# Offset stage of a convolution with deformable sampling: regroup the offsets after all the rows, and share the row copies otherwise over three DMA queues

## The reference, cut to what matters

```
x = x + L0(_gn(x))    # two 3x3 convolutions 32 -> 16, batch norm, a 3x3 attention map with a sigmoid
x = x + L1(_gn(x))    # deformable 3x3 convolution 32 -> 32
# L1, for each pixel and each of the 9 taps k:
offs = conv3x3(x, offset_w) + offset_b          # 18 channels: y and x offset of each tap
mask = 2 * sigmoid(conv3x3(x, mod_w) + mod_b)   # 9 channels
sampled = bilinear(x, y + off_y + ky, x + off_x + kx) * mask
out = einsum('nckhw,ock->nohw', sampled, w) + bias
out = relu(batch_norm(out))                     # mean and variance over images and pixels
```

## Time and profile before

| | |
|---|---|
| median of three runs | 480.02 us |
| the profiled execution | 479.59 us |
| its span in the trace | 477.8 us |
| PE busy | 344.6 us (72%) |
| DVE busy | 332.2 us (70%) |
| ACT busy | 269.0 us (56%) |
| POOL busy | 156.3 us (33%) |
| mean granted TensorE clock | 0.859 of full speed |
| sampling loop | about 194 to 436 us |

### The profile page before, as it was taken

One profiled execution on the slowest core, in us unless ns is written; L12 is line 12 of the kernel. 1 busy time (PEld: TensorE's weight loads), 2 busy tenths in 40 slices (PEclk: granted clock), 3 DMA queues, 4 the chain that ended last, 5 costly groups with the idle time before them and its releaser, 6 DMA issues.

```text
span 477.8 us, 14528 instructions
## 1 busy us (share of the span) xinstructions
PE 344.6 (72%) x6057; PEld 217.8 (46%) x6058; DVE 332.2 (70%) x625; ACT 269.0 (56%) x508; POOL 156.3 (33%) x218
## 2 busy tenths in 40 slices
PE   0089999495251933899979999979999789992550
PEld 0022334121110311677766777757777567772450
DVE  5363348806440582599995999939999599997156
ACT  1022333113210342889886989958898689893344
POOL 8910000663440000244442444414444235445100
PEclk9988999987655565999997999979999899998565
DMA  6895100575614233210000100001000000000004
GB/s 205 176 233 138 29 1 0 149 175 140 150 38 95 71 92 80 58 43 25 25 25 2 43 25 25 25 4 41 25 20 9 24 5 3 3 3 8 12 1 176
DMA packets 18707, 28.66 MB, mean 60 GB/s; under 512 B 6998, under 2 KB 7573, under 8 KB 18629
## 3 DMA queue, kind: packets, MB, share of 16 engines
q1 hardware_dynamic: 13765, 21.02, 16.5%
q0 software_dynamic: 1632, 3.45, 3.3%
q10 hardware_dynamic: 3246, 3.27, 3.0%
HBM read 8.03 MB, written 5.83 MB: 29 GB/s over the span
## 4 chain that ended last, share of the span: by engine, by line
DVE 51%; PE 22%; SPq 11%; DMA 6%; issue 4%; ACT 2%; ACTq 2%; POOL 1%; DVEq 1%; POOLq 0%
DVE prod L1309 27%; DVE areg L1317 18%; SPq L340 5%; PE ps L582 4%; PE ps L603 4%; SPq L435 4%; PE ps L652 3%; DMA prod<-xpad 2%; PE ps L593 2%; ACTq L340 2%; PE ps L780 2%; SPq L415 2%; PE ps L715 2%; DMA x_sb<-in_x 1%; PE ps L639 1%
## 5 line engine op out<-in xcount | busy, mean ns | idle before, releaser
L559 POOL TENSOR_TENSOR prod<-prod 128x288 f32<-128x288 f32 x128 | 99.9, 801 | 195.1 <-DVE prod L1309 195.1
L1309 DVE TENSOR_TENSOR prod<-ps,hy 128x480 f32<-128x480 f32 (+1 forms) x256 | 139.3, 600 | 33.7 <-PE ps L780 33.7
L780 PE MATMUL ps<-zreg,hx 64*64 64x96 f32 x4608 | 135.9, 252 | 14.9 <-DVE prod L1309 14.9
L780 PEld LDWEIGHTS ps<-zreg,hx 64*64 64x64 f32 x4608 | 112.7, 135 | 34.0 <-DVE prod L1309 26.1
L931 ACT ACTIVATE hx<-ps 128x576 f32<-128x576 f32 x131 | 78.1, 648 | 54.0 <-PE ps L771 30.2
L937 ACT ACTIVATE hx<-hx,rbias 128x576 f32<-128x576 f32 x131 | 95.6, 795 | 0.0
L1317 DVE TENSOR_REDUCE areg<-prod 128x32 f32<-128x576 f32 x128 | 92.6, 747 | 0.9 <-POOL prod L559 0.9
L639 PE MATMUL ps<-preg,sel 26*128 26x288 bf16 x260 | 44.4, 292 | 14.4 <-DMA preg<-wreg 11.7
L1013 ACT ACTIVATE zreg<-ps 128x288 f32<-128x288 f32 x128 | 46.1, 424 | 0.0
L771 PE MATMUL ps<-wzp,sreg 128*128 128x144 bf16 x512 | 44.5, 232 | 0.0
L960 ACT ACTIVATE sreg<-ps,offbc 128x512 f32<-128x512 f32 x8 | 5.5, 687 | 63.5 <-PE ps L652 42.7
(11 more groups left out here) (177 smaller groups left out, 339.3 us busy)
## 6 DMA issues: line engine op xcount, KB each, us to landing
scratch<-zreg SPq DMA_DIRECT2D x12, 240.0 KB, 4.2
sreg<-scratch SPq DMA_DIRECT2D x12, 192.0 KB, 2.5
out<-x_sb SPq DMA_DIRECT2D x8, 256.0 KB, 2.1
areg<-xpad SPq DMA_DIRECT2D x30, 66.0 KB, 2.4
x_sb<-in_x SPq DMA_DIRECT2D x3, 512.0 KB, 4.8
sreg<-scratch SPq DMA_DIRECT2D x4, 336.0 KB, 3.3
hx<-xpad SPq DMA_DIRECT2D x18, 66.0 KB, 4.0
zreg<-xpad SPq DMA_DIRECT2D x18, 66.0 KB, 2.1
```

Of the source, the lines that this page charges most:

```text
L559: pool.tensor_tensor(slots[:, :, 0:2 * KK], slots[:, :, 0:2 * KK], slots[:, :, 4 * KK:6 * KK], ALU.add).then_inc(folded, 1)
L780: return pe.matmul(g_ps(g, h)[u * W:(u + 1) * W, k - TAPS[h][0], :, :], hx[s, (t + u) % 4, k, :], z_sb[s, y + u + k // 3:y + u + k // 3 + ...
L1309: mul = vector.tensor_tensor(pv[:, n0:n1], gv, wv[:, n0:n1], ALU.mult)
```

## The change

1. Rows are numbered n = 3·b + dy, and each queue gets a range of the 12. First convolution: SP 0 to 3, ACT 4 to 7, POOL 8 to 11 (4/4/4 where it was 6/3/3). Second: SP 0 to 4, ACT 5 and 6, POOL 7 to 11 (5/2/5 where it was 6/3/3). PE's counts follow.
2. SP issues rows of 3 ahead of store 0, rows of 5 ahead of store 1, and all rows, 6 and 7 too, ahead of the first regrouping.
3. Quarters 0 and 1 are regrouped together by 9 DMAs of twice the size, when both have been saved; so there are 27 regroup DMAs in place of 36. Store 2 comes behind them. Load 0 comes next, then regroup 2 (as DMAs 10 to 18), store 3, regroup 3, and the other loads.
4. The waits on `px_ready` are counted down by 9. DVE waits once for the last split of GpSimd (xparts_low) before the sampling loop.

```diff
+        SYNC_ROWS, ACT_ROWS, POOL_ROWS = range(0, 4), range(4, 8), range(8, 12)
+        SYNC_ROWS2, ACT_ROWS2, POOL_ROWS2 = range(0, 5), range(5, 7), range(7, 12)
+
+        def replicate(eng, c, rows, homes, done):
+
+            for n in rows:
+                b, dy = n // 3, n % 3
                 r = c * CH_ROWS + PAD_T - 1 + dy
                 eng.dma_start(homes[c][dy * C:(dy + 1) * C, b, :],
                               xpad[b * C:(b + 1) * C, r:r + CH_ROWS, :].rearrange("c r x -> c (r x)"))\
-                    .then_inc((last if b == B - 1 else ready)[c], 16)
-
-        def replicate2(eng, c, b):
+                    .then_inc(done[c], 16)
+
+        def replicate2(eng, c, rows, done=rep2_ready):
 
             eng.wait_ge(norm2, c + 1)
             if REUSES[c] is not None:
                 eng.wait_ge(cv_ready, REUSES[c] + 1)
-            replicate(eng, c, b, xrep2, rep2_ready, rep2_last)
+            replicate(eng, c, rows, xrep2, done)
...
             for c in range(NCH):
                 sync.wait_ge(norm1, (c + 1) // 2 + 1)
-                replicate(sync, c, 0)
-                replicate(sync, c, 1)
+                replicate(sync, c, SYNC_ROWS, xrep, xrep_ready)
...
-            def regroup_offsets(q):
+            def regroup_offsets(q0, q1, counted, taps=range(KK)):
+
                 n = 2 * CH_ROWS * W
-                g, at = q // 2, q % 2 * n
-
-                sync.wait_ge(px_ready, 16 * (1 + q * PX_DMAS))
-                sync.wait_ge(tp_saved, q + 1 + CREDIT)
-                for k in range(KK):
-                    sync.dma_start(px[g * NXP:(g + 1) * NXP, k, at:at + n],
-                                   tpart[k * NXP:(k + 1) * NXP, q * n:(q + 1) * n]).then_inc(px_ready, 16)
+                g, at = q0 // 2, q0 % 2 * n
+
+                sync.wait_ge(px_ready, 16 * (1 + counted))
+                sync.wait_ge(tp_saved, q1 + CREDIT)
+                for k in taps:
+                    sync.dma_start(px[g * NXP:(g + 1) * NXP, k, at:at + (q1 - q0) * n],
+                                   tpart[k * NXP:(k + 1) * NXP, q0 * n:q1 * n]).then_inc(px_ready, 16)
 
             def rows_for(*chunks):
 
                 for c in chunks:
-                    for b in range(2):
-                        replicate2(sync, c, b)
-
-            rows_for(0, 1, 2)
+                    replicate2(sync, c, SYNC_ROWS2)
+
+            rows_for(0, 1, 2, 3)
             store_parts(0)
-            rows_for(3, 4)
+            rows_for(4, 5)
             store_parts(1)
-            rows_for(5)
-            regroup_offsets(0)
-            rows_for(6)
+            rows_for(6, 7)
+            regroup_offsets(0, 2, 0)
             store_parts(2)
-            rows_for(7)
-            regroup_offsets(1)
 
             sync.wait_ge(off_ready, NCH)
             sync.wait_ge(xparts_stored, 16 * B * (NQ - 1))
             load_piece(0, 0)
+            regroup_offsets(2, 3, PX_DMAS)
             store_parts(NQ - 1)
+            regroup_offsets(3, 4, 2 * PX_DMAS)
             for q in range(1, NQ):
-                if q < 3:
-                    regroup_offsets(NQ - 3 + q)
...
             for c in range(3):
-                replicate2(pool, c, B - 1)
+                replicate2(pool, c, POOL_ROWS2, rep2_last)
             pool.wait_ge(norm2, NCH)
             split_low_rows(0)
-            replicate2(pool, 3, B - 1)
-            replicate2(pool, 4, B - 1)
+            replicate2(pool, 3, POOL_ROWS2, rep2_last)
+            replicate2(pool, 4, POOL_ROWS2, rep2_last)
             split_low_rows(1)
...
-                pe.wait_ge(rep2_ready[c], 16 * 3 * (B - 1))
-                pe.wait_ge(rep2_last[c], 16 * 3)
+                pe.wait_ge(rep2_ready[c], 16 * (len(SYNC_ROWS2) + len(ACT_ROWS2)))
+                pe.wait_ge(rep2_last[c], 16 * len(POOL_ROWS2))
...
-            pe.wait_ge(px_ready, 16 * (1 + 3 * PX_DMAS))
+            pe.wait_ge(px_ready, 16 * (1 + 2 * PX_DMAS))
             distance(0, 0, PAIR_BANKS[0])
...
             for c in range(NCH // 2):
                 act.wait_ge(norm1, (c + 1) // 2 + 1)
-                replicate(act, c, 2)
+                replicate(act, c, ACT_ROWS, xrep, xrep_ready)
             root(1)
...
                 if 3 <= c + 2 < NCH:
-                    replicate2(act, c + 2, 2)
+                    replicate2(act, c + 2, ACT_ROWS2)
                 save_conv2(c)
...
             vector.wait_ge(hy_ready, NQ * 3)
+            vector.wait_ge(xparts_low, NQ)
```

More of the change, by code:

```diff
@@ L334, in conv_deform_kernel @@
         block = ctx.enter_context(nc.Block())
-        def replicate(eng, c, b, homes=xrep, ready=xrep_ready, last=xrep_last):
-            for dy in range(3):
+        SYNC_ROWS, ACT_ROWS, POOL_ROWS = range(0, 4), range(4, 8), range(8, 12)
[3 more added lines that the diff above has]
+                b, dy = n // 3, n % 3
                 r = c * CH_ROWS + PAD_T - 1 + dy
@@ L500, in _ @@
                 pool.wait_ge(norm1, (c + 1) // 2 + 1)
-                replicate(pool, c, 3)
+                replicate(pool, c, POOL_ROWS, xrep, xrep_last)
             def split_low_rows(q):
@@ L521, in _ @@
             for c in range(3):
-                replicate2(pool, c, B - 1)
+                replicate2(pool, c, POOL_ROWS2, rep2_last)
             pool.wait_ge(norm2, NCH)
             split_low_rows(0)
-            replicate2(pool, 3, B - 1)
-            replicate2(pool, 4, B - 1)
+            replicate2(pool, 3, POOL_ROWS2, rep2_last)
+            replicate2(pool, 4, POOL_ROWS2, rep2_last)
             split_low_rows(1)
-            replicate2(pool, 5, B - 1)
-            replicate2(pool, 6, B - 1)
+            replicate2(pool, 5, POOL_ROWS2, rep2_last)
+            replicate2(pool, 6, POOL_ROWS2, rep2_last)
             split_low_rows(2)
-            replicate2(pool, 7, B - 1)
+            replicate2(pool, 7, POOL_ROWS2, rep2_last)
             split_low_rows(3)
@@ L565, in _ @@
             pool.wait_ge(reach_ready, 2)
-            pool.wait_ge(px_ready, 16 * (1 + NQ * PX_DMAS))
+            pool.wait_ge(px_ready, 16 * (1 + 3 * PX_DMAS))
             far_rows(pool, lambda b, y, n: None, far_stage)
@@ L575, in conv_chunk @@
             def conv_chunk(c, u):
-                pe.wait_ge(xrep_ready[c], 16 * 3 * (B - 1))
-                pe.wait_ge(xrep_last[c], 16 * 3)
+                pe.wait_ge(xrep_ready[c], 16 * (len(SYNC_ROWS) + len(ACT_ROWS)))
+                pe.wait_ge(xrep_last[c], 16 * len(POOL_ROWS))
                 rows = xrep[c].rearrange("p b (r x) -> p b r x", x=XC)
@@ L758, in _ @@
                         if t == CH_ROWS:
-                            pe.wait_ge(px_ready, 16 * (1 + NQ * PX_DMAS))
+                            pe.wait_ge(px_ready, 16 * (1 + 3 * PX_DMAS))
                     pe.wait_ge(dist_ready, t + 3)
@@ L914, in _ @@
                     act.wait_ge(norm1, (c + NCH // 2 + 1) // 2 + 1)
-                    replicate(act, c + NCH // 2, 2)
+                    replicate(act, c + NCH // 2, ACT_ROWS, xrep, xrep_ready)
                 save_branches(c, c % 2)
@@ L971, in _ @@
             for c in range(3):
-                replicate2(act, c, 2)
+                replicate2(act, c, ACT_ROWS2)
             act.wait_ge(late_loaded, 16 * NLATE)
```

## The result

The changed kernel takes 447.57 us (median of 4 runs, 443.76 to 448.61) where the kernel before takes 478.14 (4 runs): a ratio of 0.938, 95% interval 0.927 to 0.949. That is 30.6 us less, where 25.3 were forecast; 447.6 lies in the range, near its lower end. Medians are of all runs of a kernel, ratios only of the runs in its faster state, so a ratio is not quite the quotient of two medians.

A forecast was written before the change was run, and what follows sets the result against it. Offset stage bound by waits in SP's queue, not transfer rate; the start by needed rows coming last. 22.1 us (offset stage) plus 3.2 (first convolution) make 25.3 off 479.59: 454.3 us, range 446 to 465.

The forecast's parts named there:

- (a): Start of the offset stage: chunk 0 of the second convolution starts at 94.2 us, where it was 95.44.
- (d): Offset stage: store 1 goes at 117.4 us, and chunk 6 starts at 128.1 in place of 152.95.
- (c): Offset stage: DVE's second split ends at 117.4 us, not 120.47; chunks 3, 4, 5 start at about 107.5, 115, 121.
- The sign of being wrong: Offset stage: PE waiting over 2 us for chunk 4 or 5 would show the forecast wrong.
- (e): Chunk 6 to regrouping: 7.25 us to ready for chunk 7, then 7.0; quarter 1 saved at 142.3, not 168.0.
- (f): SP's path from quarter 1's save to the first distance: 22.5 us, first distance at 164.9 where it was 186.97.
- step (b): Chunks 0 to 2 of the offset stage: chunk 2 ends at 105.6 us, DVE's first offsets 3.1 us sooner.
- The first convolution: Start of the kernel: chunk 1 starts at 27.6 us, when `attw` is made, in place of 30.80; 3.2 us.
- rival 1: Offset stage's regrouping: large regroup DMAs cost double, 6.4 us more, total 460.7 us; chance 0.10.
- rival 2: First convolution: transfer rate alone sets chunk 1, which stays at 30.80; total 457.5 us; chance 0.15.
- rival 3: Offset stage: transfers become the bound, at 150 GB/s chunk 6 starts 9.6 us later; total 463.9 us; chance 0.10.
- Rival 4: Sampling loop: low clock adds 2 us a pair; 518 us if half the loop ran so; chance 0.03.

The follow-up runs named there:

- order_only: SP's new order and the joint regrouping, with the old 6/3/3 shares in both convolutions, against the kernel before: 456.52 us, ratio 0.963.
- store_first: The changed kernel with store 2 issued ahead of the joint regrouping: 446.0 us, ratio 0.946 to the kernel before.
- split_regroup: The changed kernel with store 2 at once on SP and the regrouping spread over POOL, SP and ScalarE: 441.64 us, ratio 0.937 to the kernel before.
- before_paced2: The kernel before with 46, 80 and 16 full-size float32 matmuls on idle operands ahead of the waits for chunks 5, 6, 7: 478.96 us, ratio 1.008.
- after_again: The changed kernel run and profiled once more, unaltered: 451.16 us, ratio 0.950 to the kernel before.
- share1_only: The kernel before with rows shared 4/4/4 in the first convolution only: 472.91 us against 478.62, ratio 0.990.
- warm_start: The changed kernel with ten 512-column matmuls on loaded data ahead of the first convolution's first chunk: 451.7 us, ratio 0.950 to the kernel before.
- split_paced: `split_regroup` plus 12 matmuls ahead of the first convolution, 14 and 30 float32 ones ahead of the second's chunks 4 and 6: 440.66 us.
- before_paced: The kernel before with 30, 52 and 10 26-row matmuls on idle operands ahead of the waits for chunks 5, 6, 7: 487.58 us, ratio 1.023.

## Why the prediction was right, and where its size was off

**The cause is right.** SP's queue held ready buffers empty behind store 1 and regroup 0. With the order alone turned round, the stage is 23.7 us shorter (`order_only`). Chunk 6 was put at 41.3 us behind the second normalization and came at 41.4 and 42.6; in the first profile steps (a) to (d) each hold within 1.1 us, in the second within 1.8. In (c) DVE's split ended 1 us late: one of its casts took 1.78 us in place of 0.80 while POOL's second split ran beside it. In (d) the five rows behind the store went 1 us sooner and made it good; this was luck, for in the second profile they did not. The sign of being wrong that came true, PE waiting over 2 us for chunk 4 (4.56 and 3.33), comes from PE's pace, as the miss in (e) does: chunk 3 took 2.78 us in these profiles and not the 4.92 of before, so PE was ready sooner, and chunk 4 started no later than forecast.

**Step (f)** is right to 0.4 us: from regrouping to first distance 22.16 us in place of 22.5, with the new wait at 3.2 as written. `store_first` shows that the wait was on the path, and `split_regroup` that SP's issuing was: spread over three queues, (f) takes 12.9 us, 9.2 less, and what is left is bound by DVE's last parts to within 0.87 us.

**Step (e) was mis-sized, the main miss of the offset stage.** It said that from the start of chunk 6 to ready for chunk 7 are 7.25 us and from there to regrouping 7.0, as the rows of before show, 14.25 together. Measured: 4.36 + 4.93 = 9.3 in the first profile, 5.9 + 4.9 = 10.8 in the second. I read 5.35 and 4.81 us off as the price of a chunk. They are the price of a chunk after PE has idled 15.30 us, and of the next one, still slow after 0.84 us more: the same has chunk 1 at 2.75. With all rows sent ahead chunk 7 follows chunk 6 after at most 0.54 us, and it takes 2.78 in every profile of the new order; its turns and the parts' turning go at that pace too; chunk 6 itself is fast or slow by how long PE has waited. I used the 2.75 in step (b) and not here. That is 3.4 to 5.0 us. `before_paced2` shows it in the old order too: with chunk 7 at 2.78 regrouping starts 4.9 us behind it and not 7.0.

**The first convolution: 3.2 us forecast, 5.1 and 5.4 measured.** The new shares acted in the direction forecast, but through another number: chunk 1 did not wait for `attw` (made at 26.9, with chunk 1 at 28.2), and chunk 0 came at 23.1 and not 22.2, so chunk 1, which now only waits for PE to finish chunk 0 at its slow pace, gained only 2.6 us. The other 2.5 came behind it, where PE, with the gap of 1.55 us gone, was at its fast pace earlier. Chunk 1, the first attention product and chunk 2 took 3.58, 1.10 and 2.78 us where they had taken 4.16, 2.02 and 3.77. The sum had carried the shift through unchanged "by PE's unbroken work".

**The total.** The profile lost 35.8 us for the 25.3 of the sum. Of the 10.5 us between, 5.0 are (e), 1.9 the first convolution, 0.2 the small misses of the other steps, and 3.4 the spread behind the first distance, which is luck. In `after_again`, 28.6 us, the last is 1.4 us the other way.

**The rivals.** Large DMAs cost no more (rival 1 out: 714 ns either way). The rate does not decide chunk 1 (rival 2 out, `share1_only`). The transfers were not the bound (rival 3 out): chunk 6 was on time. That rival was priced 1.8 us low: 72 rows of 66 KB and two stores of 0.96 MB are 6.7 MB, not 6.4. From 87 to 124 us the changed kernel moved 194 GB/s. Rival 4, the slow pace in the loop, did not come in the changed kernel's first pairs, 3.04 us each; it came in other kernels, for one pair in `before_paced2`, `store_first`, `warm_start` and `split_regroup` and for two in `split_paced`, at 1.5 to 2.2 us a pair, for which I had put 2. A shorter wait is not its condition: in `warm_start` PE waited 11.57 us ahead of the first distance, about as in the kernel before.

**Joined DMAs** were priced as part of (f) with nine issues. That they save nothing against eighteen, since quarter 0's find cover, I had not seen; it changes no term of the sum.

## What to carry to other kernels

Look in a DMA-issuing queue for ready work that stands behind a wait for something later: here two such places cost 24 us of a 480 us kernel, and they show as long PE waits for a transfer that itself took 2 us. A duration read off the trace holds only under its own circumstances: if a change removes the idle time ahead of an instruction, price it by a row of the same instruction that follows work directly. After changing the waits ahead of a stage, look at the first instructions of the next stage, where the gain may be given back.

## What the runs showed of the hardware

- PE's pace follows what it did before. In all profiles the 24 matmuls of a chunk in the second convolution took 4.48 to 5.35 us when PE had idled 2.91 us or more right ahead of them. They took 2.75 to 2.78 us in most other cases, after waits of up to 2.17 us. The idle time right ahead does not decide alone: chunk 7 took 4.81 and 4.74 us after waits of 0.84 and 1.03 us (`before`, `share1_only`), with a chunk at 5.35 and over 15 us of idle time ahead of that, and chunks directly behind one at 5.35 took up to 3.68 us. The granted clock is 0.98 of full speed in the changed kernel from 118 to 134 us (its upper level, 2.4 GHz), where chunks 6 and 7 run fast, and was 0.50 (1.2 GHz) in the kernel before from 131 to 153 us.
- After back-to-back matmuls on 26 rows of bf16 the three chunks took 5.35, 5.35 and 4.75 us (`before_paced`); after matmuls on 128 rows of float32 they took 2.78 (`before_paced2`).
- SP's issue of a copy takes 0.59 us for a row of 66 KB and 0.71 for a regroup DMA of 24 or of 48 KB. Directly behind store 1 (0.96 MB) the issues of the next three rows took 1.06, 1.90 and 1.17 us in the changed kernel, 1.26, 2.48 and 0.89 in `after_again`; in the kernel before it was two, 1.54 and 2.42. POOL issued the nine large regroup DMAs in 4.99 us where SP takes 6.92.
